# A three-layer hybrid model in one kernel: q's norm moved into the exponential, longer loops, and work moved off VectorE

## What is computed

```python
qkv = x @ Wqkv                      # 128 -> 3 * 1024
q, k, v = heads(qkv)                # 16 heads of 64
q = q / max(norm(q), 1e-12) * qs    # per row and head
k = k / max(norm(k), 1e-12) * ksc
q = q*cos*scale + rotate_half(q)*sin*scale
k = k*cos/scale + rotate_half(k)*sin/scale
# windows of 32 rows, each sees the window before it and its own: 64 keys
sim = einsum(q, k) * 8;  sim = where(mask, -big, sim)
x = x + concat_heads(softmax(sim) @ v) @ Wo
x = x + (a * gelu(gate)) @ W2 + b2   # a, gate = layernorm(x) @ W1 + b1
```

## Time and profile before

| | |
|---|---|
| median of 3 runs | 4249.22 us (4222.85 to 4254.8) |
| profiled execution | 4242.4 us, its span 4240.6 us, mean granted TensorE clock 0.927 |
| busy: TensorE / its weight loads | 3627.4 us (86%) / 2575.4 us (61%) |
| busy: VectorE / ScalarE / GpSimd | 3285.6 us (77%) / 2655.0 us (63%) / 2568.1 us (61%) |
| DMA queue of SP | 241.71 MB, 23.9% of the 16 engines |

### The profile page before, as it was taken

How to read it: one execution, slowest core, us unless ns; L and a number is a source line. 1 busy time by engine, 2 the same in 40 slices (tenths; PEclk the granted TensorE clock), 3 DMA queues, 4 the chain that set the end, 5 groups by cost and what they waited for, 6 DMA issues and landing times. The chain is left out here.

```text
span 4240.6 us, 161633 instructions
## 1 busy us (share of the span) xinstructions
PE 3627.4 (86%) x62588; PEld 2575.4 (61%) x62588; DVE 3285.6 (77%) x5230; ACT 2655.0 (63%) x6841; POOL 2568.1 (61%) x2852
## 2 busy tenths in 40 slices
PE   8798889888998999896555789898998989999997
PEld 3576666666666666673111266666666666666664
DVE  7778777787877878783888788777878888787774
ACT  2467667666666767673334467666666767676664
POOL 3566666666666666660333566666666666666662
PEclk9899999999999999997787899999999999999998
DMA  1222232232322223221000122222222232322321
GB/s 37 61 64 67 67 75 61 71 71 62 74 66 66 70 67 73 66 68 23 0 0 0 26 66 67 67 71 66 70 68 70 70 72 65 73 70 66 73 62 41
DMA packets 183112, 252.06 MB, mean 59 GB/s; under 512 B 53658, under 2 KB 74782, under 8 KB 182302
## 3 DMA queue, kind: packets, MB, share of 16 engines
q1 hardware_dynamic: 182422, 241.71, 23.9%
HBM read 39.13 MB, written 1.05 MB: 9 GB/s over the span
## 5 line engine op out<-in xcount | busy, mean ns | idle before, releaser
L834 POOL TENSOR_TENSOR qk_rows<-rot_products 128x512 f32<-128x512 f32 x768 | 982.3, 1279 | 791.0 <-DVE rot_products L641 790.9
L641 DVE TENSOR_TENSOR rot_products<-psum,rot_scaled 128x1024 f32<-128x1024 f32 x768 | 936.3, 1219 | 140.8 <-ACT squares L467 108.5
L842 POOL TENSOR_TENSOR qk_rows<-qk_rows,rnorm 128x512 f32<-128x512 f32 x768 | 816.8, 1094 | 15.0
L266 PE MATMUL psum<-wqkv_hi,xs_hi 128*128 (+1 forms) x1152 | 572.7, 497 | 200.8 <-DVE rot_products L641 146.3
L467 ACT ACTIVATE squares<-psum 128x512 f32<-128x512 f32 x768 | 479.9, 625 | 219.8 <-PE psum L268 203.5
L279 PE MATMUL psum<-ident,qk_rows 128*128 128x128 f32 x3072 | 428.4, 285 | 118.8 <-issue 117.8
L643 DVE TENSOR_REDUCE sumsq<-squares 128x8 f32<-128x512 f32 x768 | 518.3, 675 | 0.0
L363 PEld LDWEIGHTS psum<-o_t,wo 128*128 128x128 f32 x3072 | 451.5, 229 | 76.9 <-ACT o_t L483 63.2
L363 PE MATMUL psum<-o_t,wo 128*128 128x128 f32 x3072 | 464.1, 315 | 25.4 <-ACT o_t L483 24.0
L279 PEld LDWEIGHTS psum<-ident,qk_rows 128*128 128x128 f32 x3072 | 376.2, 149 | 159.5 <-issue 138.7
L268 PE MATMUL psum<-wqkv_hi,xs_lo 128*128 (+1 forms) x1152 | 472.0, 410 | 0.0
(11 more groups left out here) (157 smaller groups left out, 6213.5 us busy)
## 6 DMA issues: line engine op xcount, KB each, us to landing
v_pairs<-v_rows SPq DMA_DIRECT2D x3072, 64.0 KB, 2.0
wqkv_staged<-in_Wqkv SPq DMA_DIRECT2D x52, 384.0 KB, 3.3
wo<-in_Wo SPq DMA_DIRECT2D x12, 512.0 KB, 4.6
w<-in_W SPq DMA_DIRECT2D x12, 341.0 KB, 3.7
qk_scale<-in_qk_scale SPq DMA_DIRECT2D x12, 128.0 KB, 3.3
w<-in_W SPq DMA_DIRECT2D x12, 128.0 KB
rot_base<-in_rot SPq DMA_DIRECT2D x2, 512.0 KB, 3.6
out_x<-qk_rows SPq DMA_DIRECT2D x1, 1024.0 KB, 5.1
```

The lines of the kernel that those rows point to most:

```text
L266: nc.tensor.matmul(proj_ps[c % 2], xh, wh, start=True, stop=False)
L641: V.tensor_tensor(m["mm"][:, c % 2, :, :].rearrange("p a (h e) -> p a h e", e=DH), ps, cos_sin, ALU.mult)\
L834: G.tensor_tensor(qk[:, c * CH:(c + 1) * CH].rearrange(half, a=2, e=DH // 2), cos, sin[:, :, ::-1, :], ALU.add)\
L842: G.tensor_tensor(part, part, m["rn"][:, u % 2, HC * c:HC * c + HC].unsqueeze(2) .to_broadcast([P, HC, DH]), ALU.mult).then_inc(S["rot_don ...
```

## The change

Six things, all in the stack:

1. q isn't multiplied with its inverse norm any more. GpSimd multiplies only k's two chunks; TensorE transposes q as soon as GpSimd has added its products (`add_done`). The inverse norm becomes the scale of the exponential. It differs from head to head, so the even heads too get eight instructions of 64 columns. The exponential's bias becomes minus the maximum times the inverse norm, a new VectorE product on 128x16 (`mxs`).
2. So VectorE's subtraction for the even heads (L680) and its sum of their denominators (L687) go.
3. On ScalarE, the even heads' exponential stands behind the copy to `o_t`, where it stood ahead of it.
4. The high parts of x and of the weights are made by ScalarE, their rests by GpSimd.
5. TensorE, ScalarE and GpSimd loop over layers, with four batches written out.
6. There are four `v_pairs` buffers in place of two. The transfers of a unit wait for the product with v three units earlier.

The core of the diff:

```diff
 def pe_qk_t(it, u, after, groups):
     for g in groups:
-        nc.tensor.wait_ge(S["rot_done"], cnt(it, QKC, u, g + 1))
+        if g < 2:
+            nc.tensor.wait_ge(S["add_done"], cnt(it, QKC, u, g + 1))
+        else:
+            nc.tensor.wait_ge(S["rot_done"], cnt(it, 2, u, g - 1))
...
-        def act_exp_odd(it, u):
-            nc.scalar.wait_ge(S["max_done"], cnt(it, 1, u, 1))
+        def act_exp(it, u, par):
+            nc.scalar.wait_ge(S["mxs_done"], cnt(it, 1, u, 1))
             wait(nc.scalar, S["pT_mm"], cnt(it, 2, u))
             wait(nc.scalar, S["den_done"], cnt(it, 1, u))
             for hp in range(HP):
-                last = nc.scalar.activation(m["p"][:, hp, 1, :], s_ps[1][...], ACT.Exp,
-                                            bias=m["mx"][:, 1, hp:hp + 1],
-                                            accum_out=m["den"][:, 1, hp:hp + 1])
-            last.then_inc(S["exp1_done"], 1)
-        def act_exp_even(it, u):
-            nc.scalar.wait_ge(S["sub_done"], cnt(it, 1, u, 1))
-            nc.scalar.activation(m["p"][:, :, 0, :], m["p"][:, :, 0, :], ACT.Exp)\
-                .then_inc(S["exp0_done"], 1)
+                last = nc.scalar.activation(m["p"][:, hp, par, :], s_ps[par][...], ACT.Exp,
+                                            bias=m["mxs"][:, par, hp:hp + 1],
+                                            scale=m["rn"][:, u % 2, 2 * hp + par:2 * hp + par + 1],
+                                            accum_out=m["den"][:, par, hp:hp + 1])
+            last.then_inc(S["exp1_done" if par else "exp0_done"], 1)
...
+        def act_xs(it, u):
+            t, b = u % TILES, (it + u // TILES) % B
+            wait(nc.scalar, S["qkv_mm"], cnt(it, NCH, u - 1))
+            nc.scalar.wait_ge(S["stream"], it + u // TILES + 1)
+            nc.scalar.activation(m["xh"][:, u % 2, :], xf[:, b, t * P:(t + 1) * P], ACT.Copy).then_inc(S["xs_hi"], 1)
+        def act_weights(it):
+            k = it + B
+            nc.scalar.wait_ge(S["wstaged"], (k + 1) * 16)
+            nc.scalar.activation(m["wh"][:, (k // 4) % 2, bass.ds((k % 4) * WQ, WQ)], m["wst"][:, 0, :], ACT.Copy)\
+                .then_inc(S["whi_done"], 1)
-        def act_body(it, mlp, ahead):
+        def act_body(layer, j, mlp, ahead, more):
+            it = layer * B + j
             for u in range(TILES):
+                if ahead or u + 3 < TILES:
+                    act_xs(it, u + 3)
                 if nxt:
                     act_qk_t(it, u + 1, (0, 1))
 ...
+                if u == 0 and more:
+                    act_weights(it)
 ...
                 if nxt:
-                    act_exp_odd(it, u + 1)
-                    act_exp_even(it, u + 1)
+                    act_exp(it, u + 1, 1)
                 act_out_t(it, u)
+                if nxt:
+                    act_exp(it, u + 1, 0)
                 if ahead or u + 3 < TILES:
                     act_square(it, u + 3, 1)
...
         def dve_softmax_in(it, u):
...
-            V.tensor_tensor(m["p"][:, :, 0, :], s_ps[0].rearrange(...), m["mx"][:, 0, :]..., ALU.add)
+            V.wait_ge(S["newton"], cnt(it, STEPS, u, STEPS))
+            wait(V, S["exp0_done"], cnt(it, 1, u))
+            V.tensor_tensor(m["mxs"][:, :, :], m["mx"][:, :, :], m["rn"][:, u % 2, 0:HEADS].rearrange("p (h a) -> p a h", a=2),
+                            ALU.mult).then_inc(S["mxs_done"], 1)
         def dve_den(it, u):
+            V.wait_ge(S["exp1_done"], cnt(it, 1, u, 1))
             V.wait_ge(S["exp0_done"], cnt(it, 1, u, 1))
-            V.tensor_reduce(m["den"][:, 0, :], m["p"][:, :, 0, :], AX.X, ALU.add).then_inc(S["den_sum"], 1)
...
+        def pool_xs(it, u):            # in pool_rotate, behind the addition of chunk 1
+            G.wait_ge(S["xs_hi"], cnt(it, 1, u, 1))
+            G.tensor_tensor(m["xl"][:, u % 2, :], xf[...], m["xh"][:, u % 2, :].bitcast(F32), ALU.subtract)...
+        def pool_weights(it):          # behind unit 0's pool_rotate
+            G.wait_ge(S["whi_done"], k + 1)
+            G.tensor_tensor(m["wl"][...], m["wst"][:, 0, :], m["wh"][...].bitcast(F32), ALU.subtract)...
             pool_newton(it, u)
-            for c in range(QKC):
+            for c in range(2, QKC):
...
-            with nc.tensor.Fori(max(first + 1, 2), last) as it:
-                pe_body(it, True, True)
+            with nc.tensor.Fori(layer + 1, layer + DEPTH - 1) as l:
+                for j in range(B):
+                    pe_body(l, j, True, True)
...
         def sp_pairs(it, u):
-            wait(SP, S["o_mm"], (it * TILES + (u - 1)) * 2)
+            wait(SP, S["o_mm"], (it * TILES + (u - 2)) * 2)
```

More of the change, by code:

```diff
@@ L404, in pe_body @@
                 if proj:
[L405 removed]
+                    pe_proj(it, u + 2, 2, two)
                 if prev:
@@ L583, in act_ffn @@
             last = first + PHASE - 1
+            act_xs(first, 0)
+            act_xs(first, 1)
             for u in range(2):
@@ L588, in act_ffn @@
                     act_v(first, u, c)
+                if u == 0:
+                    act_xs(first, 2)
             act_qk_t(first, 0, range(4))
             nc.scalar.preload_act_table_set("natural_log_exp_and_others")
-            act_exp_odd(first, 0)
-            act_exp_even(first, 0)
+            act_exp(first, 0, 1)
+            act_exp(first, 0, 0)
             act_square(first, 2, 0)
             act_square(first, 2, 1)
[L595 to L600, removed]
+            layer = first // B
+            for j in range(B):
+                act_body(layer, j, j > 0, True, True)
+            with nc.scalar.Fori(layer + 1, layer + DEPTH - 1) as l:
+                for j in range(B):
+                    act_body(l, j, True, True, True)
+            for j in range(B):
+                act_body(layer + DEPTH - 1, j, True, j < B - 1, j < B - 1 or first == 0)
             act_center(last)
@@ L725, in dve_down, with dve_body @@
             last_.then_inc(S["stream"], 1)
-        def dve_body(layer, j, mlp, ahead, more):
+        def dve_body(layer, j, mlp, ahead):
             it = layer * B + j
@@ L843, in pool_rotate, with pool_body @@
                                 .to_broadcast([P, HC, DH]), ALU.mult).then_inc(S["rot_done"], 1)
+        def pool_body(layer, j, ahead, more):
+            it = layer * B + j
+            for u in range(TILES):
+                if ahead or u + 2 < TILES:
+                    pool_rotate(it, u + 2, True, ahead or u + 3 < TILES)
+                else:
+                    pool_probs(it, u)
+                if u == 0 and more:
+                    pool_weights(it)
         def pool_ffn(first):
-            last = first + PHASE - 1
+            layer = first // B
             G.wait_ge(zeroed, 3)
-            for u in range(2):
-                pool_rotate(first, u, False)
-            with nc.gpsimd.Fori(first, last) as it:
-                for u in range(TILES):
-                    pool_rotate(it, u + 2, True)
-            for u in range(TILES):
-                if u + 2 < TILES:
-                    pool_rotate(last, u + 2, True)
-                else:
-                    pool_probs(last, u)
+            pool_xs(first, 0)
+            pool_xs(first, 1)
+            pool_rotate(first, 0, False, False)
+            pool_xs(first, 2)
+            pool_rotate(first, 1, False, False)
+            for j in range(B):
+                pool_body(layer, j, True, True)
+            with nc.gpsimd.Fori(layer + 1, layer + DEPTH - 1) as l:
+                for j in range(B):
+                    pool_body(l, j, True, True)
+            for j in range(B):
+                pool_body(layer + DEPTH - 1, j, j < B - 1, j < B - 1 or first == 0)
         SP = nc.sync
```

105 lines of the change are left out of this document (47 added, 58 removed).

## The result

The changed kernel takes 4461.88 us, the median of four runs (4442.97 to 4462.18), against 4252.01 for the kernel before, run beside it. The ratio is 1.0491, with a 95% interval of 1.0427 to 1.0554: slower by 4.9%. The profiled execution took 4462.14 us, 219.7 more than the 4242.4 of the one before.

The account below looks back on a forecast made before the run. TensorE's own order of work was taken as the bound. A batch going from 74.05 to 80.8 us gave +284 over 42, plus 42 and 6: 4242 + 332 = 4574, stated as 4565 us, range 4215 to 4650.

Parts of the forecast that it names:

- wait and clock: Likeliest case: TensorE waits for q's copy in every unit and its clock falls; 4480 to 4650 us, chance 0.56.
- the wait alone: Rival: TensorE waits 2.5 us a unit but its clock stays up; 4324 us (4290 to 4400), chance 0.16.
- ScalarE's chain: ScalarE's work from the first exponential to q's copy in each unit: 3.5 us longer, against 1.0 us of slack.
- The rival of the free scale: Exponentials' scale from a tile costs nothing, wait 1.05 us a unit, clock up; 4076 us (4000 to 4150), chance 0.18.
- The wait: TensorE, before transposing k, waits 2.5 us for q's copy in every unit, about 190 times, some 480 us in all.
- The clock: TensorE's clock falls behind the waits for q's copy: 4 x 1.3 = 5.2 us a batch, mean about 0.91.
- The other six batches and the jumps: Batches outside the looped 42: +7 us each, +42; the six loop jumps left: +6 us.
- The full-clock batch: A batch without clock falls: 64.3 us of TensorE's work plus 11.3 idle, 75.6 us.
- The other parts at nothing: VectorE's new product, GpSimd's and ScalarE's moved work and the four buffers were taken to add no time.
- The break-even: A batch equals today's 74.05 us at a wait of 2.1 us, a scale costing 0.065 us, with the clock up.
- The loops and VectorE's parts: Fewer loop jumps and weight parts off VectorE's path remove idle times and clock falls: up to 8.8 us, to 65.6 a batch.

Follow-up runs that it names:

- e1: The changed kernel with a constant 1.0 as scale of all sixteen exponentials, q's norm left out of the scores: 4088.68 us.
- e4: The changed kernel with the even heads' exponentials ahead of the copy to `o_t`, as in the kernel before: 4709.16 us.
- e9: The changed kernel with two v-pair buffers in place of four: 4457.29 us.
- e5: The changed kernel with q's norm back on GpSimd, the old exponentials and order, and also two v-pair buffers instead of four: 4151.93 us.
- e8: The changed kernel with a constant scale for the eight odd heads only, the even heads keeping the tile's scale: 4299.67 us.
- e2: The changed kernel with q's norm back on GpSimd and the old exponentials and order; longer loops, moved parts and four buffers stay: 3905.63 us.
- e6: The kernel of e2 with TensorE, ScalarE and GpSimd looping over batches as before: 4039.49 us.
- e7: The kernel of e2 with the parts of x and of the weights back on VectorE: 4094.26 us.

## Why the prediction was right, and where a size was off

The forecast was 4565 us in a range of 4215 to 4650, slower by over 1% with a chance of 0.72. It came out slower, for the reason given, at 103 us less than forecast. But 4462 lies in none of the ranges that I gave to single cases: below the 4480 to 4650 of wait and clock, above the 4290 to 4400 of the wait alone. It is near the middle between their 4574 and 4324, because half of the clock's price came. That the whole range holds it is owed to its width. (My sum was 4574, and nothing in it gives the step down to 4565.)

- **ScalarE's chain, +3.5 us: right.** Measured 7.73 - 4.26 = +3.47. The scale's price was taken as 0.09 an instruction; the pitch went from 0.29 to 0.38, and without the operand (e1) 373 us came back. The rule of the Trainium skill (ScalarE: Activation LUTs, What ACT_TABLE_LOAD costs), about 93 ns for each such operand, agrees with it, for the second operand too. The rival of the free scale, 4076 us, had its size right (e1 has 4089) and its condition wrong. The other steps of the chain, eight more exponentials and the high part of x, were not tested one by one.
- **The wait: right in sum, split in two.** I expected 2.5 us at one place; it was 0.4 at `o_t` and up to 2.3 at `q_t`, 2.33 a unit together (447 us over 192). The prediction said that edit 3 would end the wait for `o_t` of the earlier trace rows and otherwise doesn't help. It didn't end it: the odd heads' exponentials are 8 x 0.093 = 0.74 us dearer, the even heads' one that left the place took 0.52, and that wait went from 24.0 to 58.0 us in all. And it does help: without edit 3 the changed kernel takes 247 us more (e4). TensorE waited 183 times for `q_t`, where 190 were forecast. The idle time of a looped batch was forecast as 11.3 us and is 11.2, in part by luck: the two waits are 9.2 of it where I had 10, and the rest is 2.0 where I had 1.3.
- **The clock: the mis-sized term.** I took 4 x 1.3 = 5.2 us a batch. TensorE is busy 67.7 us a batch against 64.3 at full clock, so at most 3.4; and units 1 and 3 above, at PEclk 1.00, are 0.26 and 0.16 longer than their like in the earlier trace rows, which leaves 3.4 - 4 x 0.2 = 2.6 for the clock. The argument "2.5 us is nearly 2.9" counted a fall for nearly every wait. I count a fall where the eight transposes behind the wait (over 1.3 us instead of 1.12) or the projection chunk behind them (a matmul over 0.56 us instead of 0.4 to 0.5) were slow. Of the 121 waits for `q_t` of 2.3 us 68 had one, 56 of these in the transposes already; of the 43 of 1.8 to 2.2 us 17 had, and of the 19 shorter ones none. In e1, with 153 waits of up to 1.6 us, one had. One of the 17, where the clock falls only in the chunk:

```profile
964.48 1.12 PE L283 MATMUL psum<-ident,qk_rows 128*128 128x128 f32 x8 [1.90 <-ACT q_t L501]
965.35 0.48 PE L267 MATMUL psum<-wqkv_hi,xs_hi 128*128 x1
965.67 0.53 PE L268 MATMUL psum<-wqkv_lo,xs_hi 128*128 x1
966.00 0.63 PE L269 MATMUL psum<-wqkv_hi,xs_lo 128*128 x1
```

  In the 42 looped batches there are 76 such falls, 1.8 a batch. At the prediction's own 1.5 us each that is 2.7 us, which fits the 2.6: the price of a fall was about right and their number was not, since 5.2 us are 3.5 falls a batch. The mean clock in the loops stayed at 0.95 and 0.96; 0.91 was forecast. This is (5.2 - 2.6) x 42 = 109 us of the miss.
- **The other six batches and the jumps, +48 forecast, +18 measured.** The loops give (78.86 - 74.05) x 42 = 202 of the 219.7. No experiment took these batches apart. By the sums over 95 units, the 2 x 11 units that lie outside the stretches of 21 batches gained 19 us of idle time and lost 5 of busy time, so the falls of the clock that I had counted there too did not come; why stays open. The full-clock batch was in turn a little dearer than forecast, 65.1 + 11.2 = 76.3 for 75.6, +29 us. The three terms make up -109 - 30 + 29 = -110 of the 112 between 4574 and 4462.
- **The rival without the clock, 4324 us, was wrong**, though not much further off than the forecast (138 us against 103): the wait does cost clock, busy time 168 us above 3006. e4 is the other end: waits of mostly 3.3 to 3.6 us in one piece, and busy time 284 us above 3006.
- **The other parts at nothing in the changed kernel: right for the buffers** (e9, within the intervals), not tested for the rest. ScalarE waits only 10.3 us in all for VectorE's new product, and its 47 copies of 128x768 take 0.83 us each; TensorE waits five times for GpSimd's `qk_rows`, 15.9 us in all. That two buffers would do "with a unit 2.5 us longer" holds; it can't be turned round, as I did for e5, into their being nearly free in a fast unit.
- **The break-even.** I put it at 0.065 us an operand with the clock up. e1, e8 and the changed kernel give 4089, 4300 and 4462 us for 0, 0.047 and 0.093 on average, so 4252 is reached near 0.036, an estimate along the line between e1 and e8, which takes half of the scales at full price for all of them at half. The break-even had the clock up; at 0.047 it isn't: e8 has 103 us of busy time above 3006.
- **The loops and VectorE's parts: right.** 65.6 us a batch was what could be had; e2 has 66.7, and without these parts e6 and e7 take 134 and 189 us more than e2.

## What to carry to other kernels

Before you fold a factor into an instruction that is issued many times on another engine, price one more operand on all of them and follow that engine's order to the next buffer that the bounding engine wants; here 16 x 0.093 us and eight more instructions used up a slack of 1.0 us. A change of several parts can hide a large gain behind one bad part, so try each part alone and each part taken out. A buffer that gives nothing in a kernel with another wait may be worth 6% once that wait is gone.

## What the runs showed of the hardware

- A second operand from a tile costs an activation as much as the first. The pitch of the exponentials of 64 columns, each with its sum read out, is 0.289 us with one (before and e1) and 0.382 with two, 0.093 more; a single one costs 0.088 and 0.089 at 512 columns.
- TensorE's clock after an idle time, by the transposes and the projection chunk right behind it: a fall behind 1 of 153 waits of up to 1.6 us (e1), 17 of 43 of 1.8 to 2.2 us and 68 of 121 of 2.3 us (the changed kernel).
- Length alone does not decide. In e8 44 of the 78 waits of 1.8 to 2.2 us had a fall and only 18 of the 54 of 2.3 us or more. In the changed kernel the place in the batch goes with it: 40 of 42 waits in unit 0 had one, 26 of 47 in unit 2, 14 of 48 in unit 1 and 5 of 46 in unit 3, though 37 of those 46 were of 2.3 us. In e8 unit 3 comes first with 24 of 46. What it is about the place is not shown.
- In e4 the output projection took over 2.2 us instead of 2.05 behind 102 of 114 waits of 3.3 to 3.7 us, behind 30 of 32 of 2.2 to 2.4 us, and behind 2 of 10 of up to 1.7 us.
- e4 has 135 us more idle time than the changed kernel, and 116 us more busy time for the same work. Whether that is due to its one piece in place of two, or to the length alone, is not shown.
